# Selective scan in half positions: the drives of two states in one GpSimd instruction, and six of sixteen states weighed by GpSimd

## The chip, the cores and the metric

The kernel runs on one core of a Trainium2 chip. The metric is the device time of one execution in microseconds (us). One core has five engines that run side by side and are coupled by semaphores: TensorE (PE in the rows; PEld is its weight load), VectorE (DVE), ScalarE (ACT), GpSimd (POOL) and SyncE (SP), which issues the DMAs.

## The reference, cut to what matters

Two "metaformer" layers over four images of 384 channels and 32x32 positions. Each layer is a selective scan (a state space model) followed by a feed-forward part; that of layer 1 is a mixture of four experts.

```python
def step(h, inp):                       # layer 0: 4 directions, 384 channels, 16 states
    dtt, ut, bt, ct = inp
    dA = jnp.exp(dtt[..., None] * A)                       # decay
    h = h * dA + (dtt * ut)[..., None] * bt[:, :, None, :] # drive = (dt*u) * B
    y = jnp.einsum('bkdn,bkn->bkd', h, ct)                 # weigh with C, sum over 16 states
    return (h, y)
```

Layer 1 has the same recurrence with one direction and 768 channels. For each state n of the 16, over the positions l: `h[l] = exp(A_n dt[l]) h[l-1] + du[l] B_n[l]`, and `y = sum_n C_n h_n`. The experts compute `gelu(x w1 + b1) w2 + b2`, weighted by a gate.

## The kernel before, in words

**Images.** The first image's scans run in a function of their own (`lane_scans`), on all 1024 positions at once. All other scans run in `fused_scans`, on half the positions (512) at a time: layer 0 of an image as 24 lanes, layer 1 as 12 lanes. This happens three times (a loop body that runs twice, with names ending in `_a`, and a last image, `_b`), so there are 3 x (24 + 12) = 108 lanes. Into these stages the expert products of the image before are woven (`up`, `gelu`, `down`, `evict`).

**A lane** is 128 channels of one direction over one half, and has N = 16 steps, one for each state. A layer-0 stage takes three lanes of the first half, three of the second half, and so on; a layer-1 stage takes six and six. One step s with state n = s % 16 goes through the engines so:

- ScalarE, `decay` (L1297): the exponential of A_n times delta, written into one of SLOTS = 4 PSUM banks. It waits until the bank is free (`vacated`). Projections, sums and so on take their turn in the same ring of banks.
- GpSimd, `drive` (L1400): du times the row B_n, 128x512, into one of DRIVES = 3 buffers `dBu`. It waits for the B row (loaded two states at a time) and for `scanned`, so it is at most three steps ahead.
- VectorE, `scan` (L1449): the recurrence, from the decay in PSUM and the drive in SBUF. In the second half it starts from a carry.
- The product with C_n, `weigh`. For the states with n % 3 == 1 (1, 4, 7, 10, 13: five of sixteen) the scan writes into an SBUF buffer of a ring of three, `held`, and GpSimd weighs it (L1410), two steps later (BEHIND = 2) in its own order. In a first half it copies the last column out first, as the carry of the second half (L1408). The eleven other states stay in PSUM, and VectorE weighs them at once (L1458) into one of three `prods` buffers; their carries are copied by ScalarE (L1289).
- TensorE, `add` (L1157): four transposing products that add the weighed state to PSUM bank 0. In its order the add of a state of GpSimd stands two steps later too. After 16 adds ScalarE copies the sum (`copy_sum`, L1321, at state 3 of the next lane).

Besides, per lane: VectorE makes the next lane's `delta` after state 5 (L1430), takes a sum after state 7 (layer 0 only), and in some lanes evicts expert sums (L1485) after state 8 or 6, or multiplies a gate (L1473) after state 9. GpSimd makes the next lane's `du` at state 14 (L1389). ScalarE does two GeLUs at a time, between two table loads of 1.28 us.

**What sets the order.** Each engine's order is written out by hand as loops over s; there is no scheduler. The engines meet only at semaphores. SyncE's queue loads B with `load_b`, which waits until GpSimd has used up both rows of that buffer.

Of the kernel before, what the change touches and what calls it, by code (L numbers as in the profile page):

```python
# [806 lines left out]
def fused_scans(p, m, g, st, moved, directions, tiles, rows, guests, pattern, ending, out, following=None, turn=None, load_ahead=None,  # L807
# [41 lines left out]
    SLOTS, DRIVES, PRODS, HELD, BRING = 4, 3, 3, 3, 3  # L849
# [4 lines left out]
    BEHIND = 2  # L854
# [16 lines left out]
    def by_pool(s):  # L871
        return s % N % 3 == 1
# [51 lines left out]
    held = [m.held[:, b, :] for b in range(HELD)]  # L924
# [83 lines left out]
    with nc.Block() as block:  # L1008
        @block.sync
        def _(eng):  # L1010
# [5 lines left out]
            def load_b(b):  # L1016
                s = 2 * b
                t = group(s)
                if b >= BRING:
                    eng.wait_ge(st.dbu, s - 2 * BRING + 2)  # L1020
# [242 lines left out]
        def _(eng):  # L1263
# [9 lines left out]
            def magnitude(i):  # L1273
                eng.wait_ge(st.dt, i + 1)
                if i >= 2:
                    eng.wait_ge(st.dbu, (i - 1) * N)
                eng.activation(m.du[i % 2], bank("delta", i), ACT.Abs).then_inc(st.magnitude, 1)
# [104 lines left out]
        def _(eng):  # L1382
# [9 lines left out]
            def drive(s):  # L1392
                i, n = s // N, s % N
                b = s // 2
                if n == 0:
                    eng.wait_ge(st.du, i + 1)
                eng.wait_ge(st.b[b % BRING], 16 * (b // BRING + 1))
                if s >= DRIVES:
                    eng.wait_ge(st.scanned, s - DRIVES + 1)
                eng.tensor_tensor(m.dBu[:, s % DRIVES, :], m.du[i % 2], m.B[b % BRING][:, cols(s % 2)],  # L1400
                                  ALU.mult).then_inc(st.dbu, 1)
# [10 lines left out]
            if late is not None:  # L1412
                rest = slice(L - QUARTER, L)
                eng.tensor_copy(late.un[:, :, :], g.un[:, :, rest]).then_inc(st.aside, 1)
            for s in range(STEPS):
                i, n = s // N, s % N
                drive(s)
                if n >= BEHIND and by_pool(s - BEHIND):
                    weigh(s - BEHIND)
                if n == 14 and i + 1 < LANES:  # L1420
                    du(i + 1)

        @block.vector
        def _(eng):
# [8 lines left out]
            def scan(s):  # L1433
                flip = (lambda ap: ap[:, ::-1]) if reverse(s) else (lambda ap: ap)
                eng.wait_ge(st.decay, s + 1)
                eng.wait_ge(st.dbu, s + 1)
# [12 lines left out]
                eng.tensor_tensor_scan(flip(to), flip(slot(s)), flip(m.dBu[:, s % DRIVES, :]), initial,  # L1449
# [1257 lines left out]
def build(nc, io, out, rows, half_rows, normed, gates):  # L2707
    with ExitStack() as ctx:
# [48 lines left out]
        with ExitStack() as conv:  # L2757
# [54 lines left out]
            def half_scan_tensors(stack, name, rows_C=None):  # L2812
                if rows_C is None:
# [3 lines left out]
                    (f"half_delta_{name}", [P, HALF], F32), (f"half_du_{name}", [P, HALF], F32)])  # L2817
                named = {key[5:-len(name) - 1]: t for key, t in made.items()}
                named = dict(low=low_0, C=rows_C, carry=named["carry"], delta=[delta_0, named["delta"][:, :]],
                             du=[du_0, named["du"][:, :]])  # L2820
                return Named(m, B=[m.Bb[:, 0, :], m.Bb[:, 1, :], m.Cb[:, 0, :]],
                             dBu=m.h[:, 0:2, :].rearrange("p a (b n) -> p (a b) n", n=HALF)[:, 0:3, :],
                             held=m.h[:, 1:3, :].rearrange("p a (b n) -> p (a b) n", n=HALF)[:, 1:4, :],
# [262 lines left out]
```

## Time and profile before

| | us |
|---|---|
| median of 3 runs | 5609.17 (5603.15 to 5609.78) |
| profiled execution, its own time | 5607.85 |
| its span, first to last instruction | 5606.0 |

| engine | busy us | share of the span |
|---|---|---|
| PE | 4828.6 | 86% |
| DVE | 4445.6 | 79% |
| POOL | 3960.4 | 71% |
| ACT | 3634.0 | 65% |

The shares are means over stages of different kinds. The six stages of half-position scans last, from the first scan to the last, 720.9, 363.5, 722.0, 362.0, 721.0 and 363.2 us, together 3252.6 us. The rest is the first image's scans, the parts between the stages, and the experts of the last image at the end. A lane's length is read as the distance between its first scan and that of the next lane.

### The profile page before, as it was taken

How to read it: one execution, taken by the hardware profiler on the slowest of the kernel's cores; microseconds unless marked ns; L12 is line 12 of the kernel's file. 1: busy time of each engine (PE TensorE's matmuls, PEld its weight loads, DVE VectorE, ACT ScalarE, POOL GpSimd, SP SyncE). 2: the span in 40 equal slices, each digit the busy share in tenths (PEclk: the TensorE clock that was granted, in tenths of full speed). 3: DMA queues.
4: the chain of work that ended last, by engine and by line, in shares of the span. 5: the costliest groups of instructions: out<-in, count | busy, mean ns of one | idle time of the engine just before them, and what ended most of it. 6: DMA issues, size and time to landing. Idle time of an engine off the chain costs nothing. (4 is left out here: it accounts for less than half of the span.)

```text
span 5606.0 us, 73119 instructions
## 1 busy us (share of the span) xinstructions
PE 4828.6 (86%) x23205; PEld 3411.3 (61%) x23205; DVE 4445.6 (79%) x4529; ACT 3634.0 (65%) x5725; POOL 3960.4 (71%) x3074
## 2 busy tenths in 40 slices
PE   7888797789898887888989888888998988888998
PEld 5776546656666645555666645565666654556777
DVE  6889838959999848977999957996999975896544
ACT  5666455448887757767878857775878865775222
POOL 5888619839999818857999935894999962984111
PEclk9999999989999998998999999998999999999999
DMA  5777607737877616647788724654877842562110
GB/s 206 263 252 264 211 10 258 252 132 254 287 268 268 226 34 219 224 135 250 260 280 271 269 69 171 220 183 161 281 266 276 271 166 102 201 216 93 43 43 29
DMA packets 356676, 1104.83 MB, mean 197 GB/s; under 512 B 33210, under 2 KB 121126, under 8 KB 354872
## 3 DMA queue, kind: packets, MB, share of 16 engines
q1 hardware_dynamic: 356280, 1100.06, 56.9%
q8 instruction: 187, 3.06, 0.2%
q14 instruction: 209, 1.71, 0.1%
HBM read 1086.24 MB, written 13.68 MB: 196 GB/s over the span
## 5 line engine op out<-in xcount | busy, mean ns | idle before, releaser
L1157 PE MATMUL banks<-ident,prod 128*128 128x128 f32 x4752 | 764.9, 287 | 392.5 <-DVE prod L1458 286.6
L1157 PEld LDWEIGHTS banks<-ident,prod 128*128 128x128 f32 x4752 | 556.8, 145 | 799.1 <-DVE prod L1458 557.8
L1449 DVE TENSOR_TENSOR_SCAN banks<-banks,h 128x512 f32<-128x512 f32 x594 | 723.3, 1218 | 85.8 <-ACT banks L1297 48.5
L1400 POOL TENSOR_TENSOR h<-lane,Bb 128x512 f32<-128x512 f32 x576 | 722.8, 1272 | 57.8 <-DMA Bb<-half_rows 33.8
L1297 ACT ACTIVATE banks<-lane,A 128x512 f32<-128x512 f32 x864 | 581.1, 686 | 251.6 <-DVE prod L1458 82.4
L1229 PE MATMUL banks<-w_a,Cb 128*128 128x384 f32 x1536 | 552.2, 488 | 0.0
L1449 DVE TENSOR_TENSOR_SCAN banks<-banks,half_carry_a,h 128x512 f32<-128x512 f32 x396 | 505.5, 1277 | 8.8 <-ACT banks L1297 4.9
L1400 POOL TENSOR_TENSOR h<-half_du_a,Bb 128x512 f32<-128x512 f32 x384 | 482.7, 1275 | 14.8 <-DMA Bb<-half_rows 10.1
L1297 ACT ACTIVATE banks<-half_delta_a,A 128x512 f32<-128x512 f32 x576 | 385.3, 685 | 151.5 <-DVE lane L1430 73.7
L1217 PE MATMUL banks<-big,w_a 128*128 128x256 f32 x1728 | 435.0, 394 | 1.0 <-DMA w_a<-w_in 0.8
L1458 DVE TENSOR_TENSOR prod<-banks,half_C_a 128x512 f32<-128x512 f32 x528 | 365.3, 692 | 73.4 <-DMA half_C_a<-half_rows 2.4
L506 PE MATMUL banks<-diagonals_first,Cb 128*128 128x128 f32 x2304 | 318.1, 296 | 90.2 <-DVE h L771 39.0
L1400 POOL TENSOR_TENSOR h<-lane,Cb 128x512 f32<-128x512 f32 x288 | 362.7, 1272 | 24.8 <-DVE banks L1449 14.9
L659 ACT ACTIVATE banks<-delta_first,A 128x1024 f32<-128x1024 f32 x144 | 160.7, 1116 | 333.0 <-DVE prod L778 243.9
L506 PEld LDWEIGHTS banks<-diagonals_first,Cb 128*128 128x128 f32 x2304 | 299.7, 209 | 123.9 <-issue 120.4
L1341 ACT ACT_TABLE_LOAD x288 | 369.5, 1283 | 7.1 <-PE banks L1229 1.9
L1379 ACT ACT_TABLE_LOAD x288 | 369.5, 1283 | 5.2
L1217 PEld LDWEIGHTS banks<-big,w_a 128*128 128x128 f32 x1728 | 325.7, 198 | 61.7 <-issue 11.6
L1229 PEld LDWEIGHTS banks<-w_a,Cb 128*128 128x128 f32 x1536 | 269.7, 191 | 127.2 <-issue 12.0
L2436 POOL TENSOR_TENSOR w_lo<-raw,w_hi 128x1152 fp32r<-128x1152 f32 x32 | 89.3, 2812 | 352.8 <-ACT w_hi L2516 352.7
L1410 POOL TENSOR_TENSOR h<-h,half_C_a 128x512 f32<-128x512 f32 x240 | 305.0, 1271 | 46.6 <-DVE h L1449 36.0
L1157 PE MATMUL banks<-ident,h 128*128 128x128 f32 x2160 | 334.3, 279 | 0.0
(471 smaller groups left out, 12291.6 us busy)
## 6 DMA issues: line engine op xcount, KB each, us to landing
Bb<-half_rows SPq DMA_DIRECT2D x576, 512.0 KB, 4.3
C_first<-rows SPq DMA_DIRECT2D x288, 512.0 KB, 5.4
Cb<-half_rows SPq DMA_DIRECT2D x288, 512.0 KB, 4.4
w_a<-w_in SPq DMA_DIRECT2D x256, 576.0 KB, 6.1
w_b<-w_in SPq DMA_DIRECT2D x128, 576.0 KB, 6.2
half_C_a<-half_rows SPq DMA_DIRECT2D x128, 512.0 KB, 6.7
Bb<-rows SPq DMA_DIRECT2D x96, 512.0 KB, 5.5
half_C_b<-half_rows SPq DMA_DIRECT2D x64, 512.0 KB, 6.6
```

The lines of the kernel that those rows point to most:

```text
L506: mm = eng.matmul(in_bank(2 + 2 * (s % SLOTS), k), m.du_turned[i % 2][:, block_of(k)], diagonal(n)[:, block_of(k)], start=k % (HALF // P) ...
L659: eng.activation(to, m.delta[:, i % 2, :], ACT.Exp, scale=lanes[i].A[:, a:a + 1]).then_inc(st.decay, 1)
L1157: mm = eng.matmul(ps[:, 0, at], src[:, at], m.ident[:, :], start=n == 0 and k == 0, stop=added(s) == (i + 1) * N, is_transpose=True, skip_ ...
L1217: mm = eng.matmul(hidden(u), g.w1[:, w % WRING, k, t * P:(t + 1) * P], g.un[:, k, at], start=k == 0, stop=k == CT - 1, skip_group_check=True)
L1229: mm = eng.matmul(total(b), g.h[:, u % HRING, b * P:(b + 1) * P], g.w2[:, w % WRING, t, :], start=u % PER == 0, stop=u % PER == PER - 1, s ...
L1297: eng.activation(slot(s), m.delta[i % 2], ACT.Exp, scale=x.A(j, n)).then_inc(st.decay, 1)
L1341: eng.activation(g.h[:, u % HRING, :], hidden(u), ACT.Gelu, bias=m.vec[:, b:b + 1]).then_inc(st.gelu, 1)
L1379: eng.preload_act_table_set(EXP_LN)
L1400: eng.tensor_tensor(m.dBu[:, s % DRIVES, :], m.du[i % 2], m.B[b % BRING][:, cols(s % 2)], ALU.mult).then_inc(st.dbu, 1)
L1410: eng.tensor_tensor(h, h, m.C[:, s % N, :], ALU.mult).then_inc(st.pooled, 1)
L1449: eng.tensor_tensor_scan(flip(to), flip(slot(s)), flip(m.dBu[:, s % DRIVES, :]), initial, ALU.mult, ALU.add).then_inc(st.scanned, 1)
L1458: eng.tensor_tensor(prods[own(s) % PRODS], slot(s), m.C[:, n, :], ALU.mult).then_inc(st.prod, 1)
```

## The change

GpSimd now makes the drives of both states of a pair in one instruction: du, repeated over a dimension of two, times the two B rows that already lie side by side, 128x(2x512) into one of DRIVES = 2 buffers. A step of `drive` is now a pair b. The drive of the next pair stands at every even state, ahead of the weigh of that step, and waits until both scans of the pair that used its buffer are over. The first pair of a stage is made ahead of the loop. `du` moves from state 14 to state 12. The semaphore `dbu` counts pairs, and its waits are changed to match. GpSimd weighs the states 1, 3, 6, 8, 11 and 13. The drives lie in what were `h[0]` and `h[1]`, the held buffers in `h[2]` and a new tile `half_more`.

```diff
-    SLOTS, DRIVES, PRODS, HELD, BRING = 4, 3, 3, 3, 3
+    SLOTS, DRIVES, PRODS, HELD, BRING = 4, 2, 3, 3, 3
+    POOLED = (1, 3, 6, 8, 11, 13)
...
-    BEHIND = 2
+    BEHIND, DU_AT = 2, 12
...
     def by_pool(s):
-        return s % N % 3 == 1
+        return s % N in POOLED
...  # load_b (SP) and magnitude (ACT)
-                    eng.wait_ge(st.dbu, s - 2 * BRING + 2)
+                    eng.wait_ge(st.dbu, b - BRING + 1)
...
-                    eng.wait_ge(st.dbu, (i - 1) * N)
+                    eng.wait_ge(st.dbu, (i - 1) * PAIRS)
...  # GpSimd
-            def drive(s):
-                i, n = s // N, s % N
-                b = s // 2
-                if n == 0:
+            def drive(b):
+                i = b // PAIRS
+                if b % PAIRS == 0:
                     eng.wait_ge(st.du, i + 1)
                 eng.wait_ge(st.b[b % BRING], 16 * (b // BRING + 1))
-                if s >= DRIVES:
-                    eng.wait_ge(st.scanned, s - DRIVES + 1)
-                eng.tensor_tensor(m.dBu[:, s % DRIVES, :], m.du[i % 2], m.B[b % BRING][:, cols(s % 2)],
-                                  ALU.mult).then_inc(st.dbu, 1)
+                if b >= DRIVES:
+                    eng.wait_ge(st.scanned, 2 * (b - DRIVES + 1))
+                eng.tensor_tensor(m.dBu[b % DRIVES], over_tiles(m.du[i % 2], 2),
+                                  m.B[b % BRING].rearrange("p (r l) -> p r l", r=2), ALU.mult).then_inc(st.dbu, 1)
...
+            drive(0)
             for s in range(STEPS):
                 i, n = s // N, s % N
-                drive(s)
+                if n == DU_AT and i + 1 < LANES:
+                    du(i + 1)
+                if n % 2 == 0 and s + 2 < STEPS:
+                    drive(s // 2 + 1)
                 if n >= BEHIND and by_pool(s - BEHIND):
                     weigh(s - BEHIND)
-                if n == 14 and i + 1 < LANES:
-                    du(i + 1)
...  # VectorE, scan
-                eng.wait_ge(st.dbu, s + 1)
+                eng.wait_ge(st.dbu, s // 2 + 1)
...
-                eng.tensor_tensor_scan(flip(to), flip(slot(s)), flip(m.dBu[:, s % DRIVES, :]), initial,
+                eng.tensor_tensor_scan(flip(to), flip(slot(s)), flip(m.dBu[s // 2 % DRIVES][:, s % 2, :]), initial,
                                        ALU.mult, ALU.add).then_inc(st.scanned, 1)
...  # half_scan_tensors
-                             dBu=m.h[:, 0:2, :].rearrange("p a (b n) -> p (a b) n", n=HALF)[:, 0:3, :],
-                             held=m.h[:, 1:3, :].rearrange("p a (b n) -> p (a b) n", n=HALF)[:, 1:4, :],
+                             dBu=[m.h[:, k, :].rearrange("p (r l) -> p r l", r=2) for k in range(2)],
+                             held=[m.h[:, 2, cols(0)], m.h[:, 2, cols(1)], named_more],
```

GpSimd's order in the first lane of a layer-0 stage, before, from state 6 on. L1400 are drives (one state each), L1408 and L1410 the carry copy and the weigh, L1389 is du; `Bb` and `Cb` are the three B buffers.

```order
L1400 TENSOR_TENSOR h<-lane,Bb 128x512 x3
L1408 COPY half_carry_a<-h 128x1
L1410 TENSOR_TENSOR h<-h,half_C_a 128x512
L1400 TENSOR_TENSOR h<-lane,Cb 128x512 x2
L1400 TENSOR_TENSOR h<-lane,Bb 128x512
L1408 COPY half_carry_a<-h 128x1
L1410 TENSOR_TENSOR h<-h,half_C_a 128x512
L1400 TENSOR_TENSOR h<-lane,Bb 128x512 x2
L1389 TENSOR_TENSOR half_du_a<-half_delta_a,big 128x512
L1400 TENSOR_TENSOR h<-lane,Bb 128x512
```

The same place in the changed kernel, where L1390 is du and the weigh of state 6 comes first:

```order
L1408 COPY half_carry_a<-half_more_a 128x1
L1410 TENSOR_TENSOR half_more_a<-half_more_a,half_C_a 128x512
L1400 TENSOR_TENSOR h<-lane,Bb 128x1024
L1408 COPY half_carry_a<-h 128x1
L1410 TENSOR_TENSOR h<-h,half_C_a 128x512
L1390 TENSOR_TENSOR half_du_a<-half_delta_a,big 128x512
L1400 TENSOR_TENSOR h<-lane,Bb 128x1024
L1408 COPY half_carry_a<-h 128x1
L1410 TENSOR_TENSOR h<-h,half_C_a 128x512
L1400 TENSOR_TENSOR h<-half_du_a,Cb 128x1024
```

Between the weigh of state 8 and the drive of the pair 14/15 there is now du, and a weigh stands between almost any two drives.

VectorE's order, before, at states 5 to 8 of that lane (`SCALAR_TENSOR_TENSOR` of L1449 is the scan; one that writes `h` is a state that GpSimd weighs):

```order
L1449 SCALAR_TENSOR_TENSOR banks<-banks,h 128x512
L1458 TENSOR_TENSOR prod<-banks,half_C_a 128x512
L1430 SCALAR_TENSOR_TENSOR half_delta_a<-banks,half_du_a 128x512
L1449 SCALAR_TENSOR_TENSOR banks<-banks,h 128x512
L1458 TENSOR_TENSOR prod<-banks,half_C_a 128x512
L1449 SCALAR_TENSOR_TENSOR h<-banks,h 128x512
L1449 SCALAR_TENSOR_TENSOR banks<-banks,h 128x512
L1458 TENSOR_TENSOR prod<-banks,half_C_a 128x512
```

In the changed kernel (L1451 scan, L1460 weigh, L1432 delta):

```order
L1451 SCALAR_TENSOR_TENSOR banks<-banks,h 128x512
L1460 TENSOR_TENSOR prod<-banks,half_C_a 128x512
L1432 SCALAR_TENSOR_TENSOR half_delta_a<-banks,half_du_a 128x512
L1451 SCALAR_TENSOR_TENSOR half_more_a<-banks,h 128x512
L1451 SCALAR_TENSOR_TENSOR banks<-banks,h 128x512
L1460 TENSOR_TENSOR prod<-banks,half_C_a 128x512
L1451 SCALAR_TENSOR_TENSOR h<-banks,h 128x512
```

State 6 and state 8 are now GpSimd's and state 7 is VectorE's; one weigh of VectorE is gone in each lane.

## Rows read from the trace of the kernel before

**Rows 1.** Busy time in five lanes: us, PE, PEld, DVE, ACT, POOL, clock, DMA.
```profile
1624.90:1654.30 29.40, 27.03 (x135) 18.43 (x134) 27.09 (x29) 24.39 (x44) 28.04 (x28) 1.00 0.68 226
1654.30:1684.30 30.00, 27.50 (x136) 20.33 (x135) 28.09 (x33) 25.28 (x45) 28.11 (x28) 0.94 0.86 293
1684.30:1713.60 29.30, 25.36 (x130) 17.92 (x128) 27.84 (x29) 22.81 (x33) 27.12 (x23) 1.00 0.84 292
1535.00:1565.70 30.70, 29.43 (x137) 20.27 (x136) 29.02 (x33) 23.39 (x34) 27.64 (x23) 0.94 0.64 217
2140.40:2171.80 31.40, 26.82 (x118) 18.18 (x117) 27.60 (x29) 24.36 (x44) 28.00 (x28) 0.89 0.56 178
```

**Rows 2.** Timeline of VectorE, a first-half lane: start us, us, instruction, idle before.
```profile
1664.44 0.68 DVE L1430 SCALAR_TENSOR_TENSOR half_delta_a<-banks,half_du_a 128x512 f32<-128x512 f32 x1
1665.04 1.22 DVE L1449 TENSOR_TENSOR_SCAN banks<-banks,h 128x512 f32<-128x512 f32 x1
...
1667.00 1.21 DVE L1449 TENSOR_TENSOR_SCAN h<-banks,h 128x512 f32<-128x512 f32 x1
1668.13 0.66 DVE L2945 TENSOR_TENSOR big<-big,banks 128x512 f32<-128x512 f32 x1
1668.71 1.22 DVE L1449 TENSOR_TENSOR_SCAN banks<-banks,h 128x512 f32<-128x512 f32 x1
...
1670.67 1.14 DVE L1485 SCALAR_TENSOR_TENSOR xt_a<-banks,weights,xt_a 128x384 f32<-128x384 f32 x2
1671.72 1.22 DVE L1449 TENSOR_TENSOR_SCAN banks<-banks,h 128x512 f32<-128x512 f32 x1
...
1673.68 1.21 DVE L1449 TENSOR_TENSOR_SCAN h<-banks,h 128x512 f32<-128x512 f32 x1
...
1684.29 1.29 DVE L1449 TENSOR_TENSOR_SCAN banks<-banks,half_carry_a,h 128x512 f32<-128x512 f32 x1 [0.45 <-POOL h L1400]
```

**Rows 3.** Timeline of VectorE, a second-half lane.
```profile
1507.69 1.27 DVE L1449 TENSOR_TENSOR_SCAN h<-banks,half_carry_a,h 128x512 f32<-128x512 f32 x1
1508.88 1.27 DVE L1449 TENSOR_TENSOR_SCAN banks<-banks,half_carry_a,h 128x512 f32<-128x512 f32 x1
...
1510.89 1.28 DVE L1449 TENSOR_TENSOR_SCAN banks<-banks,half_carry_a,h 128x512 f32<-128x512 f32 x1
```

**Rows 4.** Timeline of GpSimd in the lane of rows 2.
```profile
1675.03 0.18 POOL L1408 COPY half_carry_a<-h 128x1 f32<-128x1 f32 x1 [0.67 <-DVE h L1449]
1675.29 1.27 POOL L1410 TENSOR_TENSOR h<-h,half_C_a 128x512 f32<-128x512 f32 x1
1676.52 1.27 POOL L1400 TENSOR_TENSOR h<-lane,Bb 128x512 f32<-128x512 f32 x1
...
1682.93 2.50 POOL L1400 TENSOR_TENSOR h<-half_du_a,Bb 128x512 f32<-128x512 f32 x2
```

**Rows 5.** Timeline of GpSimd in the first image's scans, 128x1024.
```profile
1002.57 2.37 POOL L726 TENSOR_TENSOR more_first<-du_first,Bb 128x1024 f32<-128x1024 f32 x1
1004.89 2.38 POOL L732 TENSOR_TENSOR h<-h,C_first 128x1024 f32<-128x1024 f32 x1
```

**Rows 6.** GpSimd copies by line: count, ns min/median/max, first and last start.
```profile
L1414 POOL COPY late_un<-big x3: 822/826/826, 1228.7 to 3853.9; 128x768 f32<-128x768 f32 x3
L1871 POOL CAST rows_C_a<-big x6: 1136/1143/1147, 1995.7 to 3317.2; 128x1152 fp32r<-128x1152 f32 x6
```

**Rows 7.** Timeline of VectorE in the layer-1 lane, the scans of states 6 and 9.
```profile
2151.07 1.22 DVE L1449 TENSOR_TENSOR_SCAN banks<-banks,h 128x512 f32<-128x512 f32 x1
...
2158.10 1.23 DVE L1449 TENSOR_TENSOR_SCAN banks<-banks,h 128x512 f32<-128x512 f32 x1 [1.91 <-ACT banks L1297]
```

**Rows 8.** ScalarE in the same lane, the decays of states 8 and 9.
```profile
2153.21 0.69 ACT L1297 ACTIVATE banks<-half_delta_a,A 128x512 f32<-128x512 f32 x1
...
2157.37 0.69 ACT L1297 ACTIVATE banks<-half_delta_a,A 128x512 f32<-128x512 f32 x1
```

**Rows 9.** The gate product on VectorE, both inputs in SBUF.
```profile
L1473 DVE TENSOR_TENSOR big<-big x18: 772/1223/1699, 2160.1 to 4939.6; 128x512 f32<-128x512 f32 x18
```

More of the change, by code:

```diff
@@ L922, in lane @@
         return directions[d], i % TILES, c
-    held = [m.held[:, b, :] for b in range(HELD)]
+    held = m.held
     prods = [m.prods[:, b, :] for b in range(PRODS)]
@@ L2816, in half_scan_tensors @@
                     (f"half_carry_{name}", [P, DT1 * N], F32),
-                    (f"half_delta_{name}", [P, HALF], F32), (f"half_du_{name}", [P, HALF], F32)])
+                    (f"half_delta_{name}", [P, HALF], F32), (f"half_du_{name}", [P, HALF], F32),
+                    (f"half_more_{name}", [P, HALF], F32)])
                 named = {key[5:-len(name) - 1]: t for key, t in made.items()}
+                named_more = named["more"][:, :]
                 named = dict(low=low_0, C=rows_C, carry=named["carry"], delta=[delta_0, named["delta"][:, :]],
```

## The prediction, written before the changed kernel ran

> **What bounds the kernel now.** I first read the page's busy shares: no engine is above 86%, so the bound has to be sought stage by stage. The change touches only the half-position scans, 108 lanes of about 30 us. So I cut the trace into lanes and took the busy time of each engine in a lane [rows 1]. The reader is to see two engines close to the whole lane: VectorE 27.1 to 29.0 of 29.3 to 31.4 us, GpSimd 27.1 to 28.1. TensorE comes near it in one lane (29.4 of 30.7), ScalarE does not.
>
> Busy time counts overlaps, so next I read start-to-start distances in the timelines. VectorE, first half: a state that it weighs itself costs 1665.04 to 1667.00 = 1.96 us, one that GpSimd weighs 1.13; delta 0.60, the taken sum 0.58, an eviction 1.05 [rows 2]. A first-half lane is 11 x 1.96 + 5 x 1.13 + 1.18 = 28.4 us of VectorE; 29.4 are measured without an eviction and 30.0 with one. In a second half the scan starts from a carry, and the steps are 2.02 and 1.19 [rows 3]: 11 x 2.02 + 5 x 1.19 + 1.18 = 29.4, measured 29.3, and 30.7 with an eviction [rows 1]. So second-half lanes run at VectorE's own pace. First-half lanes are up to 1.0 us longer: GpSimd needs 16 drives at 1.23, 5 weighs with carry copy at 1.49 and one du at 1.23 = 28.4 [rows 4], exactly as much as VectorE, and when both are full each waits for the other now and then (0.45 us ahead of one lane's first scan [rows 2]).
>
> The Trainium skill (Perfetto Trace Analysis, "GPSIMD Engine Instruction") says to time GpSimd by the spacing of starts, not by the reported duration. The trace agrees: reported 1.27, spacing 1.23 [rows 4]. By durations GpSimd's lane would come to more than its neighbours leave room for.
>
> **The change, part by part.**
>
> *VectorE.* One weigh less per lane: 1.96 - 1.13 = 0.83 us in either half, 90 us over 108 lanes. This is the whole possible gain.
>
> *GpSimd's instruction.* Two drives took 2 x 1.23 = 2.46 us. The same engine's 128x1024 product has a spacing of 2.32 [rows 5]. The new instruction has a repeated du and a two-dimensional output, which no product in this trace has. From above, the bound is 2.46 (nothing saved); from below, 2 x 1.23 less the whole part of 1.23 that is not per element: (2.32 - 1.23)/512 us per element leaves 0.14, so again 2.32. A copy whose pattern has three pieces takes 0.82 us for 768 elements, a flat one 1.14 for 1152 [rows 6]: 1.07 and 0.99 ns per element with the fixed part in both, so pieces are cheap. I take 2.32.
>
> *GpSimd's lane.* 8 x 2.32 + 6 x 1.49 + 1.23 = 28.7 in a first half: 0.3 more than before and now 1.2 above VectorE's 27.6. In a second half the copy falls away: 8 x 2.32 + 6 x 1.23 + 1.23 = 27.2 against VectorE's 10 x 2.02 + 6 x 1.19 + 1.18 = 28.5.
>
> *The two buffers.* The drive of pair p+2 waits until both scans of pair p are over. I follow what each step waits for, first half without eviction. The drive of pair 5 (states 10, 11) can start when scan 7 has ended, 0.14 us later (1674.89 to 1675.03 [rows 2, 4]). From there GpSimd has no gap: drive 5, weigh 6, drive 6, weigh 8, du, drive 7, weigh 11, next lane's drive 0, weigh 13, drive 1. That is 5 x 2.32 + 4 x 1.49 + 1.23, and the last drive is seen 0.14 late (it ends 0.04 after its spacing and VectorE starts 0.10 later, 1684.29 against 1682.93 + 1.27 [rows 2, 4]): 18.9 us. Scan 2 of the next lane waits for that drive. VectorE then runs to the end of scan 7: 1.96 + 1.13 + 1.96 + 2.56 + 1.13 + 1.22, and 0.14: 10.1. The loop closes at 29.0 us, against 29.4 now: -0.4, not -0.8. Within it scans 2 and 14 wait 0.6 to 0.8 us for a drive, which they did not before.
>
> With an eviction (after state 8) the loop that closes goes over scan 9: drive 6, weigh 8, du, drive 7, weigh 11, drive 0, weigh 13, drive 1 = 15.1, then VectorE from scan 2 to scan 9 with taken sum and eviction = 14.8. Together 29.9 against 30.0: no gain. In a second half the weighs cost 1.23, the loop is 17.9 + 10.5 = 28.4, under VectorE's 28.5: there nearly all of the gain stays.
>
> *Layer-1 lanes with a gate.* Here ScalarE sets scan 9. Its decay of state 8 waits for the bank of state 6, then come a GeLU pair and two table loads, then decay 9: scan 9 starts 7.03 us after scan 6, after a wait of 1.91 [rows 7, 8]. State 6 is now GpSimd's, so its bank is free when its scan ends, 0.83 us sooner, and scan 9 comes 0.83 sooner with it. The 1.9 us also let GpSimd catch up. I take -0.9 for these.
>
> *Stage starts.* The first scan now waits for a pair, 2.36 us instead of 1.27: 1.1 us in each of three layer-0 stages. In layer-1 stages ScalarE hides about half: 3 x 0.5. Together +5.
>
> *The gate product.* Its 18 instances take 0.77 to 1.70, mean near 1.2 [rows 9], though the shape is the same: they wait for the GpSimd instruction in progress, and that is now up to 1.1 us longer. Bounds 0 and 18 x 1.1 = 20; I take half of 1.1, +9. The rule behind it is in the Trainium skill (SBUF — State Buffer, "Who interferes with whom"): VectorE with two SBUF inputs and GpSimd lock each other out for a whole instruction. By that rule, taken as if for all of VectorE, longer GpSimd instructions would slow the scans too; the trace shows that they don't, since the scans, with one input in PSUM, keep 1.21 to 1.23 us beside a busy GpSimd [rows 2].
>
> *What costs nothing.* The B rows are given back when the pair's drive ends, 8 us ahead of their next use, about 7 before. du moves two states earlier; delta is made after state 5. The magnitude on ScalarE waits for drives of the lane before last.
>
> **The sum.** Over three images, by kind of lane (first half or second by their place, measured lengths as above):
>
> - layer 0, first half, no eviction: 15 x -0.4 = -6
> - layer 0, first half, eviction: 21 x 0 = 0
> - layer 0, second half: 21 x -0.7 = -15, and with eviction 15 x -0.8 = -12
> - layer 1, first half, 31.4-us kind: 15 x -0.9 = -13
> - layer 1, the other 21: -0.7 each but for three at -0.3: -14
> - stage starts +5, gate +9
>
> That is -46 us: of the 90 that VectorE gives up, 30 turn into waits for drives. The profiled execution's 5607.85 becomes 5562; from the median 5609.17, 1.3 above it, 5563.
>
> **Rivals.**
>
> *VectorE alone decides.* If the ends of instructions overlap more than my loop says, every lane gives its 0.83: -90 + 5, 5524 us. For it: before, first-half lanes of equal load reach 29.4 with sums of 28.4 and 28.4. Against: GpSimd's plain sum of 28.7 already forbids more than 0.7 in first halves.
>
> *The pair costs two.* With 2.46 instead of 2.32 each loop of five drives grows by 0.7: first-half lanes go to 29.7 (+0.3) and 30.5 (+0.5), second halves keep -0.3 to -0.5. Sum: +5 +10 -6 -7 -6 -7, and 14 for starts and gates: 5612, no change. Rows 5 speak against it; that no product here has such a pattern speaks for it.
>
> *Slower: the weighed states reach TensorE too late.* In my loop a weigh of GpSimd ends 1.8 to 3.4 us after the start of the scan two states on; by the same steps before it was at most 1.1 in a first half. TensorE adds in a fixed order, so the expert product behind such an add waits too, then the GeLU of ScalarE, then the decays, then the scans. Place: the GeLU pair at state 13 needs the product that stands behind the add of state 6. By my steps it is there at 19.7 us of the lane, and ScalarE, after decay 13 and a table load, asks at 20.2. The margin is 0.5 us, and in a lane where TensorE has 29.4 of 30.7 us of work [rows 1] it is gone. Behind it lie some 1.6 us until scan 14. It decides from 0.43 us per lane on (46/108). At 1 us per lane: 5563 + 108 = 5671. Against: TensorE now mostly waits for VectorE, so a delay shifts it once per lane and does not add up.
>
> **How the numbers follow.** Forecast 0.64, with its own range 5545 to 5585 (gates, starts and the 0.1 to 0.2 us per lane that the loops leave out). VectorE alone 0.12, pair costs two 0.13, slower 0.09; 0.02 for others. The range 5532 to 5612 takes in the third and most of the way to the second. The bound of what can be told from no change is 0.2%, 11 us: faster is below 5598. That is the forecast (0.63), the first rival (0.12) and a little of the second; together 0.78. The same 0.11, slower 0.11.
>
> **What would show it.** Right: drives of about 2.36 us and a spacing of 2.32; 108 weighs fewer on VectorE; in steady first-half lanes 29.0 (no eviction) and 29.9, second-half lanes 28.6 and 29.9; VectorE waits for GpSimd of 0.6 to 0.8 at scans 2 and 14 of first halves, nearly none in second halves; GpSimd's waits for B rows fewer. Wrong: first halves at 28.6 (no loop), or drives of 2.5, or waits of ScalarE's GeLU for TensorE and of TensorE for GpSimd's products, with the decays late behind them.

## The result, and the profile after

| | before | after |
|---|---|---|
| median us | 5606.16 (5595.86 to 5612.57, 6 runs) | 5628.65 (5622.48 to 5637.07, 6 runs) |
| ratio | | 1.0045, 95% [1.0031, 1.0059] |
| profiled execution, own time | 5607.85 | 5636.52 |
| its span | 5606.0 | 5634.7 |
| the six half-position stages | 3252.5 | 3271.4 |

The change made the kernel slower by 0.45%, 22 us. 46 us faster had been forecast, and 5628.65 lies outside the range. The profiled executions are 29 us apart. In them the six stages that the change touches are 19 us longer, and the idle time ahead of their first scans is 5 us longer. The first of these stages also starts late: its first scan comes at 1244.8 instead of 1230.9 us, and 13 of these 14 us lie in code that did not change. The other unchanged parts are 8 us shorter. I don't put these 13 and 8 us down to the change. TensorE does the same 5909 products in that stretch, busy for 1001.9 instead of 987.3 us, at a mean granted clock of 0.91 instead of 0.92. Over the fourteen traces of this document the first scan starts between 1225.9 us (clock 0.93) and 1244.8 (0.91). In the six stages themselves the mean granted clock is 0.96 before and after, so it does not explain their 19 us.

First the new instruction, from the page of the changed kernel (as in its part 5: busy, mean ns of one, idle before, all in us but the mean):

```profile
L1400 POOL TENSOR_TENSOR h<-lane,Bb 128x1024 f32<-128x1024 f32 x288 | 679.8, 2361 | 81.5 <-DVE banks L1451 33.8
```

It is what was forecast: 2361 ns. Two single drives took twice 1272, with a spacing from start to start of 1.23 us each. Next the waits. Two views of the scan's line, before and then after, say how long VectorE was idle ahead of a scan, how many times, and for whom (this is the whole kernel; every half-position scan is in it):

```profile
  ACT banks L1297: 56.6, 79
  POOL h L1400: 45.2, 61
```

```profile
  ACT banks L1298: 114.8, 113
  POOL h L1400: 62.6, 52
```

The reader is to see that the larger new wait is not the one for GpSimd's drives, the only one that I had worked out. It is the wait for ScalarE's decays, and it doubled. I made an account of VectorE over the six stages, from the same records: busy time by line, and idle stretches over 0.16 us by what ended them.

| us in the six stages | before | after | difference |
|---|---|---|---|
| products with C on VectorE | 818 | 743 | -75 |
| gate product | 22.1 | 40.9 | +18.8 |
| idle until ScalarE | 49.7 | 110.4 | +60.7 |
| of that at scans 9 and 14 | 40.8 | 90.2 | +49.4 |
| idle until GpSimd | 29.7 | 40.4 | +10.7 |
| idle until TensorE | 2.1 | 6.9 | +4.8 |
| the rest | | | -1 |
| the stages | 3252.5 | 3271.4 | +18.9 |

To see where the waits for ScalarE begin, I followed each one back over ScalarE's records to the last idle time over 0.16 us that was not a wait for TensorE. All 56.8 us of scan 9 in the changed kernel lead back to a decay 7 that VectorE's delta released. Of the 33.4 us of scan 14, 31.1 lead back to the product of state 10 on VectorE. Waits of ScalarE for TensorE are in these chains for 0.7 us in all.

Where that happens is plain in one lane of layer 0, a first half without eviction. Before it took 29.4 us, now 30.8. Timeline of VectorE in the changed kernel, from delta to scan 14 (start us, us, instruction, idle before):

```profile
1652.21 0.68 DVE L1432 SCALAR_TENSOR_TENSOR lane<-banks,lane 128x512 f32<-128x512 f32 x1
1652.81 1.21 DVE L1451 TENSOR_TENSOR_SCAN half_more_a<-banks,h 128x512 f32<-128x512 f32 x1
...
1656.48 1.22 DVE L1451 TENSOR_TENSOR_SCAN h<-banks,h 128x512 f32<-128x512 f32 x1
1658.68 1.23 DVE L1451 TENSOR_TENSOR_SCAN banks<-banks,h 128x512 f32<-128x512 f32 x1 [0.98 <-ACT banks L1298]
...
1660.65 1.22 DVE L1451 TENSOR_TENSOR_SCAN banks<-banks,h 128x512 f32<-128x512 f32 x1
1662.00 0.69 DVE L1460 TENSOR_TENSOR prod<-banks,half_C_a 128x512 f32<-128x512 f32 x1
...
1668.38 1.23 DVE L1451 TENSOR_TENSOR_SCAN banks<-banks,h 128x512 f32<-128x512 f32 x1 [1.48 <-ACT banks L1298]
```

The same two scans in the kernel before:

```profile
1641.77 1.23 DVE L1449 TENSOR_TENSOR_SCAN banks<-banks,h 128x512 f32<-128x512 f32 x1 [0.41 <-ACT banks L1297]
...
1650.38 1.23 DVE L1449 TENSOR_TENSOR_SCAN banks<-banks,h 128x512 f32<-128x512 f32 x1 [0.39 <-ACT banks L1297]
```

And ScalarE in that lane, changed kernel. The first four rows run from the decay of state 7 to that of state 9, the others from the decay of state 13 to that of state 14:

```profile
1652.93 0.69 ACT L1298 ACTIVATE banks<-half_delta_a,A 128x512 f32<-128x512 f32 x1 [2.18 <-DVE lane L1432]
...
1654.51 1.28 ACT L1342 ACT_TABLE_LOAD   x1
...
1656.66 1.28 ACT L1380 ACT_TABLE_LOAD   x1
1657.95 0.69 ACT L1298 ACTIVATE banks<-half_delta_a,A 128x512 f32<-128x512 f32 x1
...
1662.99 0.69 ACT L1298 ACTIVATE banks<-half_delta_a,A 128x512 f32<-128x512 f32 x1
1663.62 0.58 ACT L1272 ACTIVATE lane<-banks 44x512 f32<-44x512 f32 x1
1664.21 1.28 ACT L1342 ACT_TABLE_LOAD   x1
...
1666.36 1.28 ACT L1380 ACT_TABLE_LOAD   x1
1667.66 1.30 ACT L1298 ACTIVATE banks<-half_delta_a,A 128x512 f32<-128x512 f32 x2
```

In the kernel before, the decays of states 7, 9, 13 and 14:

```profile
1635.75 0.69 ACT L1297 ACTIVATE banks<-half_delta_a,A 128x512 f32<-128x512 f32 x1 [2.00 <-DVE lane L1430]
...
1641.04 1.30 ACT L1297 ACTIVATE banks<-half_delta_a,A 128x512 f32<-128x512 f32 x2
...
1644.98 0.69 ACT L1297 ACTIVATE banks<-half_delta_a,A 128x512 f32<-128x512 f32 x1 [0.17 <-DVE h L1449]
...
1649.65 0.69 ACT L1297 ACTIVATE banks<-half_delta_a,A 128x512 f32<-128x512 f32 x1
```

*Scan 9.* Decay 7 takes the bank in which delta's input lay, so ScalarE starts it when delta is done. Then decay 8, a table load, two GeLUs, a table load and decay 9 follow without a gap. From decay 7 to decay 9 it is 5.02 us (5.29 before, with one more carry copy between). This chain does not get shorter when VectorE weighs one state less. Between scan 6 and scan 9 VectorE now has 4.9 instead of 5.7 us of work, since states 6 and 8 are both GpSimd's, and it waits 0.98 instead of 0.41.

*Scan 14.* In this lane the projection takes a turn in the ring of four banks, so decay 13 needs the bank of state 10. Before, state 10 was GpSimd's: its bank was free when scan 10 ended, and decay 13 started 1.24 us after scan 10 had started. Now it is VectorE's own: the weigh (1662.00) and ScalarE's carry copy come first, and decay 13 starts 2.34 us after scan 10. Both times scan 14 starts 5.40 us after decay 13. So it comes 1.1 us late by the bank, and VectorE waits 1.48 instead of 0.39. Lanes in which a projection takes such a turn have 28 of the 33 us at scan 14, and 10 of 11 in the kernel before.

The next lane, a first half with an eviction, shows the wait that had been forecast, in its place and of its size. VectorE and GpSimd there:

```profile
1697.74 1.23 DVE L1451 TENSOR_TENSOR_SCAN banks<-banks,h 128x512 f32<-128x512 f32 x1 [0.65 <-POOL h L1400]
```

```profile
1690.24 2.37 POOL L1400 TENSOR_TENSOR h<-lane,Bb 128x1024 f32<-128x1024 f32 x1 [0.86 <-DVE banks L1451]
...
1695.28 2.36 POOL L1400 TENSOR_TENSOR h<-lane,Cb 128x1024 f32<-128x1024 f32 x1
```

The gate product, the counterpart of [rows 9]:

```profile
L1475 DVE TENSOR_TENSOR big<-big x18: 700/2304/2595, 2177.5 to 4969.6; 128x512 f32<-128x512 f32 x18
```

### The profile page after: what moved, and what is told of

It is laid out like the page before. It is cut to its first block and busy times, and to the rows that moved or that the text cites. A ratio compares the mean times of both kernels' runs of the same rounds, so it can differ in the third digit from the quotient of the medians.

```text
span 5634.7 us, 71355 instructions
## 1 busy us (share of the span) xinstructions
PE 4841.2 (86%) x23205; PEld 3408.3 (60%) x23205; DVE 4397.5 (78%) x4421; ACT 3624.4 (64%) x5671; POOL 3983.8 (71%) x2372
## 5 line engine op out<-in xcount | busy, mean ns | idle before, releaser
L1158 PE MATMUL banks<-ident,prod 128*128 128x128 f32 x4320 | 689.4, 284 | 217.2 <-DVE prod L1460 151.7
L1158 PEld LDWEIGHTS banks<-ident,prod 128*128 128x128 f32 x4320 | 519.0, 144 | 565.0 <-DVE prod L1460 331.9
L1451 DVE TENSOR_TENSOR_SCAN banks<-banks,h 128x512 f32<-128x512 f32 x540 | 657.8, 1218 | 132.7 <-ACT banks L1298 74.5
L1400 POOL TENSOR_TENSOR h<-lane,Bb 128x1024 f32<-128x1024 f32 x288 | 679.8, 2361 | 81.5 <-DVE banks L1451 33.8
L1230 PE MATMUL banks<-w_a,Cb 128*128 128x384 f32 x1536 | 556.8, 491 | 0.0
L1400 POOL TENSOR_TENSOR h<-half_du_a,Bb 128x1024 f32<-128x1024 f32 x192 | 453.8, 2365 | 43.3 <-DVE banks L1451 22.1
L1451 DVE TENSOR_TENSOR_SCAN banks<-banks,half_carry_a,h 128x512 f32<-128x512 f32 x360 | 459.8, 1277 | 30.8 <-ACT banks L1298 26.8
L1460 DVE TENSOR_TENSOR prod<-banks,half_C_a 128x512 f32<-128x512 f32 x480 | 332.0, 692 | 65.8 <-DVE banks L1451 2.0
L1400 POOL TENSOR_TENSOR h<-lane,Cb 128x1024 f32<-128x1024 f32 x144 | 340.0, 2361 | 59.3 <-DVE banks L1451 26.1
L1230 PEld LDWEIGHTS banks<-w_a,Cb 128*128 128x128 f32 x1536 | 273.9, 193 | 129.4 <-issue 15.3
L1218 PEld LDWEIGHTS banks<-big,w_a 128*128 128x128 f32 x1728 | 318.8, 198 | 50.1 <-issue 11.6
L1158 PE MATMUL banks<-ident,h 128*128 128x128 f32 x1728 | 273.3, 282 | 58.1 <-POOL h L1410 55.5
L524 PE MATMUL banks<-ident,prod 128*128 128x128 f32 x1584 | 216.8, 285 | 90.6 <-DVE prod L778 90.2
```

The lines of the kernel that those rows point to most:

```text
L524: mm = eng.matmul(in_bank(0, k), src[:, block_of(k)], m.ident[:, :], start=s == first_add[i] and k % (HALF // P) == 0, stop=place[s] == al ...
L1158: mm = eng.matmul(ps[:, 0, at], src[:, at], m.ident[:, :], start=n == 0 and k == 0, stop=added(s) == (i + 1) * N, is_transpose=True, skip_ ...
L1218: mm = eng.matmul(hidden(u), g.w1[:, w % WRING, k, t * P:(t + 1) * P], g.un[:, k, at], start=k == 0, stop=k == CT - 1, skip_group_check=True)
L1230: mm = eng.matmul(total(b), g.h[:, u % HRING, b * P:(b + 1) * P], g.w2[:, w % WRING, t, :], start=u % PER == 0, stop=u % PER == PER - 1, s ...
L1400: eng.tensor_tensor(m.dBu[b % DRIVES], over_tiles(m.du[i % 2], 2), m.B[b % BRING].rearrange("p (r l) -> p r l", r=2), ALU.mult).then_inc(s ...
L1451: eng.tensor_tensor_scan(flip(to), flip(slot(s)), flip(m.dBu[s // 2 % DRIVES][:, s % 2, :]), initial, ALU.mult, ALU.add).then_inc(st.scann ...
```

## The experiments

Theory A: which states GpSimd weighs decides, because ScalarE's decays for scans 9 and 14 stand at a fixed distance behind VectorE's delta and behind the bank of state 10. Theory B: the two pair buffers hold the lanes up (the loop of the prediction). Theory C: GpSimd's longer instructions cost by themselves (gate, late products for TensorE). Each run is compared with the kernel before on its own chip, and two runs with each other by their distances to it; the changed kernel is 22.5 us slower by this measure. Waits and stage lengths come from one profiled execution of each kernel.

**Pair drives, five states.** From the changed kernel:

```diff
-    POOLED = (1, 3, 6, 8, 11, 13)
+    POOLED = (1, 4, 7, 10, 13)
```

> The pair drives, two buffers and du at state 12 stay, GpSimd weighs 1, 4, 7, 10, 13 again. Theory A (which state frees the bank that ScalarE's decay ahead of a GeLU pair waits for decides; the new six put VectorE's own state 10 there and shorten VectorE's way from state 5 to 9): VectorE's waits for the decays at states 9 and 14 fall back from 57 and 33 us to about 30 and 11. The gate products stay long (41 us in all, as in the changed kernel, against 22 before), since the GpSimd instruction is still 2.3 us. Six stages about 3252 + 19 + up to 10 for drives = 3270 to 3282 us; the time about 5615 to 5630. Theory B (the two pair buffers are what costs): the waits for drives stay at 40 us or more and the time stays at or above 5629. Theory C (late adds on TensorE): the decay waits at 9 and 14 stay near 57 and 33.

Measured: 5622.49 against 5605.13, 1.0029 [1.0018, 1.0041]. With five states the pair drives, together with du at state 12, cost 17 us; 11 of these are in the six stages and 5 ahead of their first scans. VectorE's idle until ScalarE is 51.5, as before (49.7), and until GpSimd 14.0 instead of 29.7: the pair does relieve the drives. The gate product takes 37.6 instead of 22.1. The time is inside what I expected, the six stages (3263.8 us) are below it. And a wait came that no theory had. The eviction's line (L1487) in this kernel:

```profile
its engine sat idle before it (us, times) until:
  PE banks L1230: 17.4, 9
```

No other run has more than 6.2 us of these waits. Eight of the nine lead back over TensorE to the same place. At 1502.03 the eviction waits for a `down` product (L1230), which stands in TensorE's order behind the add of a state of GpSimd. That add waits for GpSimd's weigh, and the weigh stands behind a drive that waited for its B rows. TensorE's add, and GpSimd's drive:

```profile
1499.05 0.66 PE L1158 MATMUL banks<-ident,half_more_a 128*128 128x128 f32 x4 [1.99 <-POOL half_more_a L1410]
```

```profile
1495.17 2.36 POOL L1400 TENSOR_TENSOR h<-lane,Cb 128x1024 f32<-128x1024 f32 x1 [2.04 <-DMA Cb<-half_rows]
```

Ahead of its drives GpSimd waits 75.4 us for B rows in this kernel, 57.7 in the kernel before and 47.6 in the changed one. Why the rows are late here was not tested.

**Six states, single drives.** From the kernel before:

```diff
-        return s % N % 3 == 1
+        return s % N in (1, 3, 6, 8, 11, 13)
```

> The kernel before, with GpSimd weighing 1, 3, 6, 8, 11, 13. Single drives, three buffers. Theory A: the decay waits at states 9 and 14 grow as in the changed kernel (to about 57 and 33), the gate stays at 22 us. GpSimd has 16 x 1.23 + 6 x 1.49 + 1.23 = 29.8 us in a first-half lane, so the waits for drives grow to 40 to 60. Six stages 3252 - 90 + 45 (decays) + 20 to 40 (drives) = 3227 to 3250, or more if the GpSimd bound of 29.8 binds in all 54 first-half lanes. Theory B: without the pair buffers the gain of 90 comes through: stages about 3200. Theory C: as A, but TensorE's waits for GpSimd's products stay near 58 us.

Measured: 5643.72 against 5605.13, 1.0079 [1.0061, 1.0097]. Idle until ScalarE is 117.0 us, 58.8 of it at scan 9 and 33.7 at scan 14: the changed kernel's 56.8 and 33.4. These waits belong to the list of states and not to the pair instruction or its buffers. Idle until GpSimd is 60.1 us. The six stages take 3283.7 us, above the 3227 to 3250 that I expected. With six states the pair is worth 16 us (from 38.6 above the kernel before to 22.5).

**State 10 for state 11**, and **states 5 and 10 for 6 and 11.** Both from the changed kernel:

```diff
-    POOLED = (1, 3, 6, 8, 11, 13)
+    POOLED = (1, 3, 6, 8, 10, 13)
```

```diff
-    POOLED = (1, 3, 6, 8, 11, 13)
+    POOLED = (1, 3, 5, 8, 10, 13)
```

> The changed kernel with state 10 instead of 11 among GpSimd's six. VectorE's and GpSimd's work is the same. Theory A: the bank of state 10 is free 1.1 us sooner, so the decay wait at state 14 falls from 33 us to about 11 and the time falls by about 20 us, to about 5608. Theories B and C: no change beyond 5 us (5629).

> The changed kernel with states 5 and 10 instead of 6 and 11. Theory A: in layer 0 the bank of state 5 is freed 0.8 us sooner and VectorE has one more weigh of its own between 5 and 9, so the wait at 9 nearly vanishes in layer 0 (from 57 to about 30 in all, the rest in layer 1 where the bank of state 6 counts and the wait grows by 0.3 to 0.8 in some lanes). Time 5595 to 5610, below e3. Theories B and C: 5629 as the changed kernel, within 5 us.

Measured: 5611.80, 1.0018 [1.0007, 1.0029], and 5578.04, 0.9952 [0.9936, 0.9969], both against 5605.13. With state 10 the wait of scan 14 for ScalarE falls from 33.4 to 7.5 us, the wait of scan 9 stays (56.1), and that of scan 14 for a drive grows from 22.2 to 30.5. With state 5 in place of 6 the wait of scan 9 falls to 25.8 too, all of it in layer 1; 19.3 of it lead back to the product of state 6 on VectorE. The number of states and the pair instruction are the same, and the kernel is 50 us faster than the changed one. I had expected 5595 to 5610, so the second list gives more than I had put on theory A. In the lane shown above, ScalarE in the last kernel:

```profile
1629.80 1.30 ACT L1298 ACTIVATE banks<-half_delta_a,A 128x512 f32<-128x512 f32 x2 [1.32 <-DVE lane L1432]
...
1634.83 0.69 ACT L1298 ACTIVATE banks<-half_delta_a,A 128x512 f32<-128x512 f32 x1
...
1638.77 0.69 ACT L1298 ACTIVATE banks<-half_delta_a,A 128x512 f32<-128x512 f32 x1 [0.17 <-DVE h L1451]
```

and VectorE, scan 9 and scan 14:

```profile
1635.55 1.23 DVE L1451 TENSOR_TENSOR_SCAN banks<-banks,h 128x512 f32<-128x512 f32 x1
...
1644.41 1.23 DVE L1451 TENSOR_TENSOR_SCAN banks<-banks,h 128x512 f32<-128x512 f32 x1 [0.63 <-POOL h L1400]
```

From decay 7 to decay 9 it is again 5.03 us. But delta now comes earlier in VectorE's own order, as the weigh of state 5 is no longer ahead of it, and that of state 6 lies behind it: VectorE is busy while the chain runs, and scan 9 does not wait. Decay 13 starts 1.24 us after scan 10 (1637.53) again. What is left at scan 14 in this lane is the drive; over the six stages scan 14 waits 21.2 us for drives and 13.4 for ScalarE. Theory A holds.

**Without the GeLUs**, on the kernel before and on the changed one. A plain copy with bias stands in their place, and the two table loads around each pair of them are gone:

```diff
-                eng.activation(g.h[:, u % HRING, :], hidden(u), ACT.Gelu,
+                eng.activation(g.h[:, u % HRING, :], hidden(u), ACT.Identity,
...
-                    eng.preload_act_table_set(EXP_LN)
```

> The kernel before, with the GeLU of the fused stages left out: a plain copy with bias in its place, so that ScalarE loads no tables around it (2 x 1.28 us less per pair of units). Theory A (ScalarE's decays decide at states 9 and 14): VectorE's waits for decays fall from 50 us to under 15, six stages 3252 - 35 to - 45, time 5560 to 5575. Theory B (the pair buffers cost the gain): the same for this kernel, the two differ in the next run.

> The changed kernel with the same cut as the run before. Theory A: with the tables gone, VectorE's weigh less per lane comes through. Its decay waits fall from 110 us to under 30; what stays against the cut kernel before is the gate's +19 us and 10 to 20 us of waits for drives: 20 to 50 us faster than that one, about 5520 to 5545. Theory B: it stays slower than the cut kernel before, by up to 20 us, with the waits for drives above 60.

Measured: 5554.86, 0.9900 [0.9880, 0.9920], and 5560.05, 0.9917 [0.9900, 0.9934], against 5609.55. The first is 5 us below the range that I gave. My expectation that the changed kernel would then be 20 to 50 us ahead missed: the two are level. ScalarE is out of the way (idle until it: 5.7 and 16.9 us), but VectorE then waits for drives. The scan's line in the changed kernel without GeLUs:

```profile
  POOL h L1399: 97.9, 103
  ACT banks L1298: 26.6, 12
```

In the six stages it is 80.6 us until GpSimd, 48.5 of it at scan 14 and 15.1 at scan 2, the places that theory B names. With the kernel before cut in the same way it is 35.4 us. So B is not a rival of A but a second limit behind it: taking away one uncovers the other.

**A third pair buffer**, on the list 1, 3, 5, 8, 10, 13, and then on the changed kernel's own list. In layer-0 stages `prod[:, 2, :]` lies idle and can hold it; the layer-1 stages keep two:

```diff
-    SLOTS, DRIVES, PRODS, HELD, BRING = 4, 2, 3, 3, 3
+    SLOTS, PRODS, HELD, BRING = 4, 3, 3, 3
+    DRIVES = len(m.dBu)
...
-                             dBu=[m.h[:, k, :].rearrange("p (r l) -> p r l", r=2) for k in range(2)],
+                             dBu=[t.rearrange("p (r l) -> p r l", r=2) for t in [m.h[:, 0, :], m.h[:, 1, :]] + ([m.prod[:, 2, :]] if name.endswith("0") else [])],
```

> States 1, 3, 5, 8, 10, 13 with pair drives, and a third pair buffer in layer-0 stages (in an unused part of prod). The drive of a pair can then start one pair sooner. VectorE's waits for drives at states 14 and 2 (21 and 10 us with two buffers) fall below 12 in all. Loop theory of the prediction: 10 to 20 us faster than with two buffers (5558 to 5568). Rival (GpSimd's plain sum of 28.7 us binds in first halves whatever the buffers): under 6 us.

> The changed kernel, its six states kept, with a third pair buffer in layer-0 stages. Loop theory: the waits for drives at states 14 and 2 (22 and 6 us) go. ScalarE theory: what they give is taken back by the decays at 9 and 14 (57 and 33 us now), since these stand at a fixed distance behind VectorE's delta and its state 10; the time falls by less than 12 us, to 5617 to 5629. Were the buffers the main cause, it would fall below 5606.

Measured: 5545.76 against 5609.55, 0.9888 [0.9872, 0.9905], and 5608.59 against 5602.35, 1.0011 [1.0001, 1.0020]. On the better list the buffer gives 37 us, all in layer 0 (2137.3 to 2099.5 us in the stages), and the drive wait of scan 14 falls from 21.2 to 9.7. I had expected 10 to 20. On the changed kernel's list it gives 16 us (22 in the stages of the profiled executions), more than the 12 that I had put as the limit. I had read its worth off the waits for GpSimd, which fell from 40.4 to 25.4 us. It stays slower than before, though, as scans 9 and 14 still wait 57.6 and 34.5 us for ScalarE. The list alone gave 50 us and the buffer alone 16; together they give 86.

**The gate product on GpSimd**, after state 9 in its order, on the list 1, 3, 5, 8, 10, 13:

```diff
                 if n >= BEHIND and by_pool(s - BEHIND):
                     weigh(s - BEHIND)
+                if i in gated and n == GATE_AT:
+                    gate(i - 1)
...
-                    if i in gated and n == GATE_AT:
-                        gate(i - 1)
```

> States 1, 3, 5, 8, 10, 13 with pair drives, and the gate product (18 in all) on GpSimd after state 9 instead of VectorE. The gate took VectorE 41 us with pair drives and 22 with single ones. If VectorE waits there for the GpSimd instruction in progress, the 41 us go and GpSimd gets 18 x 1.23 = 22 us, in layer-1 first-half lanes that wait 1.9 us for a decay right before. Gain 10 to 30 us against the same kernel with the gate on VectorE (5578): 5550 to 5568. Rival: those lanes are set by ScalarE and the loop of drives, and nothing comes of it (5573 to 5583).

Measured: 5551.92 against 5609.55, 0.9899 [0.9881, 0.9916]; 30 us less than with the gate on VectorE, the upper end of what I expected. Only 14 of these lie in the six stages of the profiled executions (3218.5 to 3204.6 us). The rest lies in code that the edit does not touch, so I count the gate at 14. In the kernel with the gate on VectorE all 18 gates take about 2.30 us:

```profile
L1475 DVE TENSOR_TENSOR big<-big x18: 2298/2302/2311, 2150.1 to 4910.3; 128x512 f32<-128x512 f32 x18
```

On GpSimd:

```profile
L1416 POOL TENSOR_TENSOR big<-big x18: 1259/1266/1276, 2141.6 to 4886.9; 128x512 f32<-128x512 f32 x18
```

41.5 us go from VectorE, and the waits for GpSimd rise from 44.8 to 65.0. Theory C holds for the gate. For TensorE it is right that GpSimd's products come late. These are TensorE's adds of them, in the changed kernel:

```profile
L1158 PE MATMUL banks<-ident,h 128*128 128x128 f32 x1728 | 273.3, 282 | 58.1 <-POOL h L1410 55.5
L1158 PE MATMUL banks<-ident,half_more_a 128*128 128x128 f32 x576 | 94.0, 287 | 91.2 <-POOL half_more_a L1410 90.3
L1158 PE MATMUL banks<-ident,half_more_b 128*128 128x128 f32 x288 | 48.3, 293 | 44.8 <-POOL half_more_b L1410 44.4
```

And in the kernel before:

```profile
L1157 PE MATMUL banks<-ident,h 128*128 128x128 f32 x2160 | 334.3, 279 | 0.0
```

So TensorE waits 190 us for GpSimd's products, and waited for none before. Still, VectorE's idle time until TensorE is only 6.9 us, and the chains to scans 9 and 14 hold 0.7 us of waits for TensorE. With states 5 and 10 in the list TensorE waits 249 us for these products, and that kernel is 50 us faster than the changed one.

**Third buffer and gate together**, and two other lists with these:

```diff
-    POOLED = (1, 3, 5, 8, 10, 13)
+    POOLED = (1, 3, 5, 9, 10, 13)
```

```diff
-    POOLED = (1, 3, 5, 8, 10, 13)
+    POOLED = (1, 3, 5, 10, 13)
```

> States 1, 3, 5, 8, 10, 13, third pair buffer in layer 0, gate product on GpSimd. The two edits touch different stages (layer 0; layer 1), so their gains add: six stages 3182 - 14 = 3168, time 5520 to 5535.

> As the run before, with state 9 instead of 8 among the six: 1, 3, 5, 9, 10, 13. ScalarE theory: scan 9 stands 6.0 us behind delta (decays 7 and 8, the GeLU pair, decay 9), so a state between 6 and 8 that GpSimd weighs gains nothing there. With 8 back on VectorE and 9 on GpSimd the decay wait at 9 falls from 25 us to about 10, time 5 to 15 us below the run before. Rival: two GpSimd states in a row (9 and 10) make its weighs late, the waits for drives grow, no gain or a loss.

> As e10 with only five states for GpSimd: 1, 3, 5, 10, 13. VectorE has 0.83 us more per lane, 90 us in all; the decay wait at 9 should almost vanish (-25) and the waits for drives too (-35 to -50). If six are worth it, this is 15 to 45 us slower than e10; if GpSimd's load is the binding one in first halves, it is level with it.

Measured, all against 5602.35: 5531.74, 0.9871 [0.9854, 0.9887]; with state 9 for 8, 5539.42, 0.9886 [0.9870, 0.9903]; with five states, 5572.88, 0.9951 [0.9934, 0.9968]. The first is the best kernel here, 1.3% faster than the one before and 93 us faster than the changed one. To the kernel with the third buffer the gate on GpSimd adds 7 us (12 in the stages). State 9 for 8 cuts the wait of scan 9 to 12.0 us, but 24.4 us come up at scan 12. I had expected 5 to 15 us from it; it is 8 us behind, with intervals that overlap: a chain moved, not a gain. Five states have only 10.5 us at scan 9 and are 41 us slower. So the sixth state on GpSimd, the idea of the change, is worth 41 us in this kernel, where the list and the third buffer have cut the waits for decays and drives.

## Why the prediction was wrong

The step that failed is *The two buffers*, with what follows for second halves: "there nearly all of the gain stays". I closed the loop over VectorE and GpSimd alone, because ScalarE does not come near the whole lane [rows 1]. So the sum let 30 us of the gain turn into waits for GpSimd, and nothing into waits for ScalarE. Measured, VectorE's waits for GpSimd grew by 10.7 us and those for ScalarE by 60.7. A share of busy time does not show such a chain: ScalarE has 6 us of unbroken work between delta and scan 9, and 5.4 between decay 13 and scan 14. Both stand beside VectorE's work of nearly the same length in the kernel before. I saw this for the layer-1 lanes alone [rows 7, 8]. In the second halves of layer 0, the largest miss, the waits for GpSimd went from 0.3 us to none, as forecast. Those for ScalarE went from 3.5 to 24.8 us.

By the terms of the sum, lane lengths after less before (in each kind all lanes of the three images; the last lane of a stage ends at its last scan, and is left out of the medians):

| kind of lane | forecast us | measured us | medians before, after |
|---|---|---|---|
| layer 0, first half, no eviction (15) | -6 | +13.9 | 29.63, 30.79 |
| layer 0, first half, eviction (21) | 0 | -5.2 | 29.94, 29.63 |
| layer 0, second half (36) | -27 | +0.4 | without eviction 29.34, 29.71; with one 30.69, 30.67 |
| layer 1, first half, the 31.4-us kind (15) | -13 | +3.0 | 31.42, 31.32 |
| layer 1, the other 21 | -14 | +6.8 | |
| gate | +9 | +18.8, inside the two rows above | |

- *VectorE, -90.* Right in number: 108 products fewer. Busy time falls by 75; the other 15 were the gaps of 0.14 us between a scan and its product. They should have gone too, but the rest in the account is -1, not -15. Stretches of up to 0.16 us fell by 8.6 us only (156.4 to 147.8). In the second halves of layer 0, for one, scan 14 now waits 0.12 to 0.15 us for its decay in 24 lanes that the account counts as free of waits there. The other 7 us are busy time outside the first two rows of the table.
- *The instruction, 2.32.* Right, spacing 2.31. The rival by which a pair costs two is out.
- *Stage starts, +5.* Right. These waits lie ahead of a stage's first scan and so outside these lengths. The idle time there grew by 1.1, 0.9 and 1.1 us in layer 0 and by 0.5 in each layer-1 stage, 4.6 in all.
- *The loop of two buffers.* The waits at scans 2 and 14 are there, 0.65 at scan 14 in the lane with an eviction. Such lanes came out shorter than the loop said: 29.63 in the median, 14 of 21 between 29.3 and 29.8, instead of 29.9. In the lanes without an eviction, but for the first of each stage, ScalarE was later than the drive at scan 14, and drives cost 3.8 us at scan 2 alone. Once ScalarE is out of the way the loop costs more than forecast: without GeLUs the change takes the waits for GpSimd from 35.4 to 80.6 us, 45 more where 30 had been forecast.
- *Layer-1 lanes with a gate, -0.9.* What I said of ScalarE was right. The counterpart of [rows 7, 8] in the changed kernel, VectorE:

```profile
2169.42 1.21 DVE L1451 TENSOR_TENSOR_SCAN half_more_a<-banks,h 128x512 f32<-128x512 f32 x1
...
2175.56 1.23 DVE L1451 TENSOR_TENSOR_SCAN banks<-banks,h 128x512 f32<-128x512 f32 x1 [1.85 <-ACT banks L1298]
...
2177.53 2.30 DVE L1475 TENSOR_TENSOR big<-big 128x512 f32<-128x512 f32 x1
```

From scan 6 to scan 9 it is 6.14 us instead of 7.03. This lane gained nothing all the same (31.7 instead of 31.4), as the gate took 2.30 and a drive came 0.49 late at scan 2.

- *Gate, +9.* Mis-sized by half: +18.8, close to the bound of 20. The mechanism was right. GpSimd beside the gate above:

```profile
2176.93 2.35 POOL L1400 TENSOR_TENSOR h<-half_du_a,Cb 128x1024 f32<-128x1024 f32 x1 [1.21 <-DVE banks L1451]
2179.23 0.64 POOL L1408 COPY half_carry_a<-h 128x1 f32<-128x1 f32 x1
```

The gate starts 0.60 us into a drive and ends 0.55 us after it. I took half of the extra length, as if gates met drives at chance. They don't, and the rows before could have told: there 12 of the 18 gates start 0.60 us into a drive. Scan 9 waits, is weighed, and the gate follows right behind, while scan 9's end is what the drive of the pair waits for. So 17 of the 18 gates start 0.3 to 0.6 us after a drive. The rule of the Trainium skill (SBUF — State Buffer, "Who interferes with whom") is that a VectorE instruction with two SBUF inputs and GpSimd's reads lock each other out for a whole instruction; these rows agree.
- *The slower rival.* Its first two signs came. TensorE's waits for GpSimd's products went from 0 to 190 us, and ScalarE's waits for TensorE at its GeLU pairs from 11.6 to 22.9. The third, the decays late behind them, did not: 0.7 us in the chains to scans 9 and 14. The place it named, scan 14, was one of the two, but by the bank of state 10.
- *What costs nothing.* For the B rows this held: GpSimd's waits for them ahead of drives fell from 57.7 to 47.6 us, though there are 49 instead of 42.

What stays open: why B rows come late with five pooled states and pair drives, and why the granted clock was lower ahead of the first stage in the profiled execution.

## What to carry to other kernels

When work is taken from the busiest engine, walk the operands of each of its steps back, not only the one that the change touches: an engine at 65% can hold a chain (table load, GeLU, table load, decay) that just fits beside the work that is taken away. Place the states that go to another engine so that the first engine is busy while that chain runs, and so that a bank is given back early where a chain behind it starts. Two limits that lie one behind the other can be worth more when both go than each alone (here 86 us against 50 and 16), so try them together before an idea is dropped.

## What the runs showed of the hardware

- GpSimd's product with a first input repeated over a dimension of two and a two-dimensional output takes 2.36 us for 128x1024, as the plain one does [rows 5].
- The lock at the gate works on both engines. GpSimd's copy of one column takes 0.64 to 0.65 us beside the gate and 0.19 us otherwise. The one gate that started ahead of a drive (at 2240.00) took 0.70 us, and the drive 2.81 instead of 2.36; the other 17 took 2.30 to 2.60. In the kernel before, three gates started 0.18 us ahead of a drive: they took 0.77 to 0.78 us, and the drives 1.72 instead of 1.27.
- The first-half scans keep 1.20 to 1.23 us with drives of 2.36 us, as with drives of 1.27.
- TensorE's same 5909 products ahead of the first half-position scan kept it busy for 987.3 us at a mean granted clock of 0.92 and for 1001.9 at 0.91.
